# A 16-head, 64-dim cross-attention with query and key weights folded per head, and bias rows added by GpSimd

## The reference, cut to what matters

```
x = x + tanh(g_xattn[0]) * L0_xattn(layernorm(x), ctx)   # 16 heads of 8, biases
x = x + tanh(g_ffn[0])   * L0_ffn(layernorm(x))          # 8 experts, top 2
x = x + tanh(g_xattn[1]) * L1_xattn(layernorm(x), ctx)   # 16 heads of 64
x = x + tanh(g_ffn[1])   * L1_ffn(layernorm(x))          # 8 small experts, thresholded
x = x + tanh(g_xattn[2]) * L2_xattn(layernorm(x), ctx)   # one head of 128
x = x + tanh(g_ffn[2])   * L2_ffn(layernorm(x))          # 8 experts, top 1
x = x + tanh(g_xattn[3]) * L3_xattn(layernorm(x), ctx)   # 16 heads of 8, biases
x = x + tanh(g_ffn[3])   * L3_ffn(layernorm(x))          # ternary weights
```

```
def L1_xattn(x, context):            # HEADS = 16, DIM_HEAD = 64
    q, k, v = x @ Wq, context @ Wk, context @ Wv       # 128x1024, 96x1024, 96x1024
    sim = einsum('bhid,bhjd->bhij', heads(q), heads(k)) * 64 ** -0.5
    out = einsum('bhij,bhjd->bhid', softmax(sim), heads(v))
    return merged(out) @ Wo + bo
```

## Time and profile before

| what | value |
|---|---|
| median of 3 runs | 857.47 us (855.55 to 860.73) |
| the profiled execution, its own time | 856.33 us |
| its span, first to last instruction | 854.5 us |
| mean granted TensorE clock | 0.901 |
| PE, PEld busy | 712.4 us (83%), 599.3 us (70%) |
| DVE, ACT, POOL busy | 473.5 us (55%), 401.1 us (47%), 304.7 us (36%) |
| chain that ended last: PE, DVE, issue, DMA, ACT, POOL | 65%, 16%, 5%, 5%, 5%, 3% |
| `heads8(0)`, `experts(0)` on PE | from about 22 us, 140 to 263.7 us |
| `heads64` on PE | 263.7 to about 492 us |
| `heads8(1)` on PE | about 687 to 806 us |

### The profile page before, as it was taken

How to read it: one execution, slowest core, us unless ns; L and a number is a source line. 1 busy time by engine, 2 the same in 40 slices (tenths; PEclk the granted TensorE clock), 3 DMA queues, 4 the chain that set the end, 5 groups by cost and what they waited for, 6 DMA issues and landing times.

```text
span 854.5 us, 17772 instructions
## 1 busy us (share of the span) xinstructions
PE 712.4 (83%) x6653; PEld 599.3 (70%) x6653; DVE 473.5 (55%) x1439; ACT 401.1 (47%) x965; POOL 304.7 (36%) x256
## 2 busy tenths in 40 slices
PE   4698896499895898898999998885699749998873
PEld 3477783399895797796988843653699647787663
DVE  5365768432236767656656577446433425668662
ACT  4465440156562563554546565311346635555640
POOL 4443513556243371220312247203153354243121
PEclk9999996599997999999999999865699858999997
DMA  6442833756862010000000020004357444320000
GB/s 170 127 109 61 239 109 109 220 150 201 245 197 71 16 33 4 1 2 0 2 1 2 1 75 1 1 1 134 92 164 224 128 101 126 86 63 2 2 26 25
DMA packets 60544, 70.88 MB, mean 83 GB/s; under 512 B 7036, under 2 KB 40717, under 8 KB 60461
## 3 DMA queue, kind: packets, MB, share of 16 engines
q1 hardware_dynamic: 57389, 63.45, 26.2%
q0 software_dynamic: 3072, 6.30, 2.6%
HBM read 48.82 MB, written 20.91 MB: 82 GB/s over the span
## 4 chain that ended last, share of the span: by engine, by line
PE 65%; DVE 16%; issue 5%; DMA 5%; ACT 5%; POOL 3%; SPq 0%; POOLq 0%; DVEq 0%; ACTq 0%
PE banks L1375 7%; PE banks L1391 6%; PE banks L1460 4%; PE banks L1192 4%; PE banks L1469 3%; PE banks L1106 3%; PE banks L1215 3%; PE banks L1480 3%; PE banks L1064 3%; PE banks L1204 3%; PE banks L1170 3%; PE banks L1065 2%; PE banks L1066 2%; PE banks L1513 2%; DVE xn L1712 2%
## 5 line engine op out<-in xcount | busy, mean ns | idle before, releaser
L914 ACT ACTIVATE hT<-banks,wup 128x128 f32<-128x128 f32 x304 | 86.5, 368 | 75.8 <-PE banks L1375 74.9
L844 ACT ACTIVATE pT<-banks 77x512 f32<-77x512 f32 x128 | 69.0, 589 | 61.9 <-PE banks L1192 61.6
L582 POOL TENSOR_TENSOR kbd<-k,const 96x1248 fp32r<-96x1248 f32 x32 | 72.8, 2284 | 59.5 <-PE banks L1192 56.9
L620 POOL TENSOR_TENSOR sh<-sh,rd 128x616 f32<-128x616 f32 x32 | 38.9, 1216 | 134.1 <-DVE rd L1750 134.1
L1375 PE MATMUL banks<-xTs,wup 128*128 128x128 f32 x608 | 84.3, 285 | 2.0 <-ACT hT L914 1.2
L660 POOL DMA_INDIRECT xs<-xn,slot x48 | 47.3, 985 | 101.7 <-DVE slot L1996 48.4
L1391 PE MATMUL banks<-wd,hT 128*128 x608 | 80.8, 276 | 0.5 <-ACT hT L914 0.4
L1375 PEld LDWEIGHTS banks<-xTs,wup 128*128 128x128 f32 x608 | 77.7, 201 | 2.7 <-issue 2.5
L1391 PEld LDWEIGHTS banks<-wd,hT 128*128 128x128 f32 x608 | 74.0, 192 | 1.0 <-issue 0.9
L2103 DVE COPY ysb<-banks 128x128 f32<-128x128 f32 x76 | 22.1, 291 | 93.6 <-PE banks L1391 93.5
L562 POOL TENSOR_TENSOR rstd<-vv,const 128x4 f32<-128x4 f32 x24 | 24.4, 1016 | 128.6 <-DVE vv L1702 126.8
(11 more groups left out here) (318 smaller groups left out, 1643.0 us busy)
## 6 DMA issues: line engine op xcount, KB each, us to landing
wup<-in_up SPq DMA_DIRECT2D x76, 258.0 KB, 3.4
q<-queries SPq DMA_DIRECT2D x24, 256.0 KB, 4.6
queries<-qc SPq DMA_DIRECT2D x8, 512.0 KB, 2.6
wd<-in_down SPq DMA_DIRECT2D x8, 512.0 KB, 5.9
ys<-ysb SPq DMA_DIRECT2D x16, 256.0 KB
k<-keys SPq DMA_DIRECT2D x24, 156.0 KB, 3.5
...
```

Source lines behind the costliest of these rows:

```text
L582: pool.tensor_tensor(kbd[b % NB8][0:96, :, :, :].bitcast(F32R), kb, m, ALU.mult).then_inc(h8.kbd, 1)
L844: act.activation(pT[b % 2][0:SK, u, :], ps[0:SK, 2 + u % 2, :], ACT.Exp, scale=D8 ** -0.5)\
L914: ins = act.activation(hT[T % 3][:, c, :], ps[:, T % 2, c * P:c * P + P], func, bias=wup[T % NW][:, HID + c:HID + c + 1])
```

## The change

It has four parts.

1. **Folded weights.** Scores are x Wq_h (c Wk_h)^T = x (Wq_h Wk_h^T) c^T. In the second half of `experts(0)`, `folded_weights(j)` of PE, behind tiles 3 and 10, makes for each of the 16 heads the 96x128 product from transposed raw weights (64 deep, float32; even heads lie in partitions 0 to 63, odd ones in 64 to 127). ACT copies the high parts out behind tiles 5, 6, 12, 13, DVE the low parts behind 7, 8, 14, 15. POOL now splits only the value weights, at move 8.
2. **Folded keys.** `folded_keys(g, part)` makes for each head a 128x312 block from the folded weights and the context (three float32r matmuls), without x. Even heads are copied out by DVE, odd ones by ACT, into one of two buffers k1. Group 0's stand at the stage's start; group g+1's stand in step 0 of group g, behind each half of `own_values`. The scores of a unit are one float32 matmul of 128x312, with the plain transposed x as weights. q1, its matmuls and copies, xhi, xlo and `front_c` of this stage, and the memset of k1 go. k1 of the next group must be copied out before the scores of batch 1.
3. **Order of `heads64`.** The group's `front` runs one group ahead, behind the last `project`; nothing stands any more between the last `values` and `project`. On DVE `last_rows` (group 0) and `front_a` stand at step 4 ahead of `add`, `front_b` at step 5.
4. **Bias rows.** The ones-row matmul of `project` goes in both `heads8` runs (32 in all) and in `heads64` (16). POOL multiplies the bias row by tanh(g) once for each layer and adds it to a group's x (`bias_rows`, a 128x512 add, 12 in all) once that group's xn is written; DVE's first `add` of a group waits for it. The bias is loaded broadcast to all partitions.

```diff
-PLAIN = (*range(3 * NG, 5 * NG),)
+PLAIN = (*range(2 * NG, 5 * NG),)
...
-            for i, n in enumerate(("q", "k", "v")):
-                rows = P if i == 0 else DC
-                sp.dma_start(l1raw[0:rows, i, :], a["L1_xattn_W" + n]).then_inc(ld.l1raw, 16)
+            sp.dma_start(wqT[:, :, :], a["wqT"]).then_inc(ld.l1raw, 16)
+            sp.dma_start(wkT, a["wkT"]).then_inc(ld.l1raw, 16)
+            sp.dma_start(l1raw[0:DC, 2, :], a["L1_xattn_Wv"]).then_inc(ld.l1raw, 16)
...
+    def bias_rows(g, n, rows):
+        pool.wait_ge(fr.xn, upto(n))
+        xt = x[:, GB * g:GB * g + GB, :]
+        pool.tensor_tensor(xt, xt, rows.unsqueeze(1).to_broadcast([P, GB, D]), ALU.add).then_inc(h8.b, 1)
...
+            if b == 0:
+                if run == 0:
+                    pool.wait_ge(su.tanh, 1)
+                pool.tensor_scalar(rows, rows, tg[:, 0, 3 * run:3 * run + 1], None, ALU.mult).then_inc(su.zero, 1)
+                pool.wait_ge(su.zero, 4 + 2 * run)
+                bias_rows(0, NG * phase, rows)
+            if b % GB == 1 and b // GB < NG - 1:
+                bias_rows(b // GB + 1, NG * phase + b // GB + 1, rows)
...
-                if hh == 1 and m in (4, 8, 12):
-                    split_l1(m // 4 - 1)
+                if hh == 1 and m == 8:
+                    split_values()
...
-    pool.wait_ge(mo.tr, BASE[2])
-    pool.wait_ge(mo.scat, moves(2))
-    pool.memset(k1[:, :, :, :, :], 0.0).then_inc(su.scratch, 1)
+    rsqrt_front(2 * NG + 1)
     for g in range(NG):
-        rsqrt_front(g + 2 * NG + 1)
+        if g == 0:
+            pool.wait_ge(ld.l1raw, 96)
+            pool.tensor_scalar(bo[:, :], bo[:, :], tg[:, 0, 1:2], None, ALU.mult).then_inc(su.zero, 1)
+            pool.wait_ge(su.zero, 5)
+        bias_rows(g, 2 * NG + g, bo[:, :])
         for b in range(GB):
             for half in range(2):
                 if g == 0:
                     collect(1, 2 * b + half, 8)
                 normalise(h64, g, b, half)
-    rsqrt_front(3 * NG + 1)
+        rsqrt_front(g + 2 * NG + 2)
...
+        def folded_keys(g, part):
+            for h in range(8 * part + 1, 8 * part + 9, 2):
+                act.wait_ge(h64.kmm, H * g + h + 1)
+                copy(k1[g % 2][:, h, :, :].rearrange("p b t -> p (b t)"), ps[:, 2 + h % 4, 0:GB * SP]).then_inc(h64.q, 1)
...
-            pe.matmul(o_, oT8[:, :], a_raw[:, 3 * P:4 * P], start=True, stop=False)
-            pe.matmul(o_, const[0:1, C_ONE:C_ONE + P], a_raw[0:1, 4 * P:5 * P], start=False, stop=True)\
-                .then_inc(h8.y, 1)
+            pe.matmul(o_, oT8[:, :], a_raw[:, 3 * P:4 * P], start=True, stop=True).then_inc(h8.y, 1)
...
+    def folded_weights(j):
+        pe.wait_ge(ld.l1raw, 64)
+        if j == 0:
+            pe.wait_ge(mo.xb, 4)
+        else:
+            pe.wait_ge(su.lo, NG + 2)
+        for h in range(8 * j, 8 * j + 8):
+            rows = slice(64 * (h % 2), 64 * (h % 2) + 64)
+            at = h % 8 // 2 * P
+            ins = pe.matmul(ps[0:DC, 2 + h % 2, at:at + P], wkT[rows, h // 2, :], wqT[rows, h // 2, :],
+                            start=True, stop=True)
+        ins.then_inc(h64.qmm, 1)
     def heads64():
-        pe.wait_ge(wr.l1, 3)
-        def blocks(g, between):
-            pe.wait_ge(fr.lo, upto(g + 2 * NG))
+        pe.wait_ge(wr.l1, 1)
+        pe.wait_ge(su.lo, 2 * NG)
+        pe.wait_ge(mo.scat, moves(2))
...
+        def folded_keys(g, part):
             ct = tuple(c_[0:DC, GB * g:GB * g + GB, :].rearrange("p b t -> p (b t)") for c_ in (chi, clo))
-            for c in range(C1):
-                if c >= 4:
-                    pe.wait_ge(h64.q, 8 * g + c - 3)
-                split3(ps[:, c % 4, :], tuple(w_[:, 0, c * P:c * P + P] for w_ in l1w), xs).then_inc(h64.qmm, 1)
-                if c >= 2:
-                    pe.wait_ge(h64.k, 8 * g + c - 1)
-                split3(ps[:, 4 + c % 2, 0:GB * SP], tuple(w_[0:DC, 1, c * P:c * P + P] for w_ in l1w), ct)\
-                    .then_inc(h64.kmm, 1)
-            between()
+            for h in range(8 * part, 8 * part + 8):
+                if h % 8 >= 4:
+                    pe.wait_ge(h64.q if h % 2 else h64.k, 8 * g + h // 2 - 1)
+                elif g:
+                    pe.wait_ge(h64.v, 8 * g - 7 + 4 * part + h % 8)
+                elif part:
+                    pe.wait_ge(h64.q if h % 2 else h64.k, h // 2 - 1)
+                split3(ps[:, 2 + h % 4, 0:GB * SP],
+                       tuple(w_[0:DC, h // 8, (h % 8) * P:(h % 8) * P + P] for w_ in l1w), ct).then_inc(h64.kmm, 1)
         def own_values(g, part):
             for i in range(4 * part, 4 * part + 4):
-                if i >= 4:
+                if i >= 4 and g < NG - 1:
+                    pe.wait_ge(h64.q if i % 2 else h64.k, 8 * (g + 1) + i // 2 + 1)
+                elif i >= 4:
                     pe.wait_ge(h64.v, 8 * g + i - 3)
                 split3(ps[0:SK, 2 + i % 4, :], tuple(c_[0:DC, GB * g + i // 2, 0:SK] for c_ in (chi, clo)),
                        tuple(w_[0:DC, 2, 512 * (i % 2):512 * (i % 2) + 512] for w_ in l1w)).then_inc(h64.vmm, 1)
+            if g == 0 and part == 0:
+                front(2 * NG + 1)
+            if g < NG - 1:
+                folded_keys(g + 1, part)
         def scores(g, b, u):
             if b == 0 and u == 0:
                 pe.wait_ge(h64.k, 8 * g + 8)
                 pe.wait_ge(h64.q, 8 * g + 8)
-                pe.wait_ge(fr.lo, upto(g + 2 * NG + 1))
+                pe.wait_ge(fr.lo, upto(g + 2 * NG))
             if b == 1 and u == 0:
                 pe.wait_ge(h64.v, 8 * g + 8)
+                if g < NG - 1:
+                    pe.wait_ge(h64.k, 8 * g + 16)
+                    pe.wait_ge(h64.q, 8 * g + 16)
+                pe.wait_ge(fr.lo, upto(g + 2 * NG + 1))
                 if g == NG - 1:
                     pe.wait_ge(mx.d, 1)
-            for i in range(2):
-                ins = pe.matmul(ps[:, u % 2, 2 * i * SP:2 * (i + 1) * SP], q1[:, 2 * u + i, b * P:b * P + P],
-                                k1[:, 2 * u + i, b, :, :].rearrange("p h t -> p (h t)"), start=True, stop=True)
-            return ins
+            return pe.matmul(ps[:, u % 2, 0:4 * SP].rearrange("p (h t) -> p h t", h=4),
+                             xT[(g + 2 * NG) % 2][:, b * P:b * P + P], k1[g % 2][:, 4 * u:4 * u + 4, b, :],
+                             start=True, stop=True)
...
             pe.wait_ge(ld.l1raw, 96)
             pe.wait_ge(h64.oT, 2 * (4 * g + b) + 2)
             for c in range(C1):
-                pe.matmul(ps[:, 6, 0:P], oT[:, c, :], wo1[:, c, :], start=(c == 0), stop=False)
-            pe.matmul(ps[:, 6, 0:P], const[0:1, C_ONE:C_ONE + P], bo[:, :], start=False, stop=True)\
-                .then_inc(h64.y, 1)
-        blocks(0, lambda: None)
-        front(2 * NG + 1)
+                ins = pe.matmul(ps[:, 6, 0:P], oT[:, c, :], wo1[:, c, :], start=(c == 0), stop=(c == C1 - 1))
+            ins.then_inc(h64.y, 1)
+        folded_keys(0, 0)
+        folded_keys(0, 1)
+        front(2 * NG)
         for g in range(0, NG - 1):
-            attend(h64, g, scores, own_values, values, project, lambda between: blocks(g + 1, between))
+            attend(h64, g, scores, own_values, values, project)
...
-    def attend(hs, G, add, prepare=None, between=None):
+    def attend(hs, G, add, folded_keys, between, prepare=None):
-            if i == GB and between:
+            if i == GB:
                 between()
-                wait_done(dve, "ff", 1)
...
+                    if i == 0 and G < NG - 1:
+                        folded_keys(G + 1, pair)
...
-        def blocks(g, between):
-            n = g + 2 * NG + 1
-            gn = next_group(g)
-            front_a(gn, n)
-            for c in range(C1):
-                if c == 0:
-                    dve.wait_ge(su.scratch, 2)
-                dve.wait_ge(h64.kmm, 8 * g + c + 1)
-                for par in range(2):
-                    rows = slice(64 * par, 64 * par + 64)
-                    ins = dve.tensor_copy(k1[rows, c, :, par, :],
-                                          ps[rows, 4 + c % 2, 0:GB * SP].rearrange("p (b t) -> p b t", b=GB))
-                ins.then_inc(h64.k, 1)
-                if c == 1:
-                    front_b(gn, n)
-            between()
+        def folded_keys(g, part):
+            if g == 1 and part == 0:
+                dve.wait_ge(mo.ys, 16 * stores(2))
+            for h in range(8 * part, 8 * part + 8, 2):
+                dve.wait_ge(h64.kmm, H * g + h + 1)
+                dve.tensor_copy(k1[g % 2][:, h, :, :].rearrange("p b t -> p (b t)"), ps[:, 2 + h % 4, 0:GB * SP])\
+                   .then_inc(h64.k, 1)
         def add(g, b):
             dve.wait_ge(h64.y, 4 * g + b + 1)
+            if b == 0:
+                dve.wait_ge(h8.b, NG + g + 1)
             add_to_x(g * GB + b, 1, ps[:, 6, 0:P], tg[:, 0, 1:2], h64.x)
-        blocks(0, lambda: None)
-        front_c(2 * NG + 1)
+        def stats(g):
```

(14 more changed lines are left out.)

85 lines of the change are left out of this document (54 added, 31 removed).

## The result

The changed kernel takes 819.61 us (median of 4 runs, 817.99 to 821.95) against 857.53 for the kernel before (4 runs): ratio 0.956, 95% interval 0.951 to 0.960. The forecast was 821.4. The profiled execution took 817.99 us, 38.3 less than the profiled one of before (856.33).

A forecast was written before the change was run, and what follows sets the result against it. PE was taken as the bound, busy 83% of the span. Terms -9.8 - 33.0 + 20.4 + 0.5 - 5.3 + 1.4 - 11.0 + 1.9 sum to -34.9 from the profiled 856.33 us, giving 821.4 us, range 809 to 838.

The forecast's parts named there:

- start of `heads64`: Experts' end to first scores: folded keys start without x, xn takes 1.1 us; -9.8 us, bounds -7.5 and -12.
- three passages: Between a group's last `values` and the next scores: only oT copy wait, `project` and transposes stay; -33.0 us.
- three first batches (with the moved transposes): Groups 0 to 2, step 0: 48 key matmuls each, +20.4 us; group 1's transposes moved into group 0, +0.5 us.
- other batches: bias matmul, statistics ahead of `add`: `heads64`: 13 bias matmuls of 0.41 us gone, -5.3 us; longer wait for `add` in group 0's step 4, +1.4 us.
- bias matmul, `heads8`: Both `heads8` runs: 32 matmuls of 0.42 us gone, 25 counting fully; -11 us, bounds -5 and -15.
- experts: folding, earlier row moves: Experts' stage: 16 folding matmuls cost +3.8 us, the wait for rows nearly goes, -1.9 us; together +1.9 us.
- The rival of the copies: First batches: DVE and ACT bring keys late, PE stands some 4 us more in each of three; 833 us, chance 0.13.
- The rival that this matmul was hidden: `heads8`: ACT and DVE chains do not pass through the ones-row matmul, so -11 becomes 0; 832 us, chance 0.08.
- the bound of 1.9: Experts' stage: folding matmuls in different row groups run at the same time, costing 1.9 us instead of 3.8.
- GpSimd's adds: Bias adds and row scalings on GpSimd hold up VectorE's xn; at most 15.2 us, 837 us, chance 0.09.
- The rivals of the low clock (slower than before): `heads64`: added idle pieces keep PE's clock low; half the stage low would give 911 us; chance 0.02.
- a change that does less: Whole kernel: less gain than said, or an unseen wait takes most back; within 0.5% of before, chance 0.02.

The follow-up runs named there:

- run 5: Changed kernel with GpSimd's 4.25 us memset put back later in the 64-dim stage, behind a wait for the 16th folded key; ratio to the kernel before 0.961.
- run 4: Changed kernel with GpSimd's 4.25 us memset back at its old place in GpSimd's order, over the second key buffer; ratio to the kernel before 0.959.
- Run 6: Changed kernel with the next group's folded keys made between last `values` and last `project` instead of in the first batch; ratio to the kernel before 0.955.
- Run 3: Kernel before with only the bias part: GpSimd adds the bias rows, the 48 1-deep matmuls gone; 833.75 us, ratio to the kernel before 0.978.
- Runs 1 and 2: Changed kernel with a zero-adding matmul in each of 48 projections, 1-deep in the first, 128-deep in the second; ratios to the kernel before 0.991 and 0.965.
- run 7: Changed kernel with all 16 folding matmuls reading partitions 0 to 63, leaving the odd heads' weights out; ratio to the kernel before 0.956.

## Why the prediction was right

Term by term, profiled execution against profiled execution:

| term | predicted | measured |
|---|---|---|
| start of `heads64` | -9.8 | -10.5 |
| three passages | -33.0 | -30.1 |
| three first batches (with the moved transposes) | +20.9 | +18.9 |
| other batches: bias matmul, statistics ahead of `add` | -3.9 | -4.4 |
| bias matmul, `heads8` | -11.0 | -16.2 |
| experts: folding, earlier row moves | +1.9 | +2.9 |
| stages not touched | 0 | +1.2 |
| sum | -34.9 | -38.3 |

The time is near the forecast (819.6 against 821.4) partly by luck: four terms gave 8.4 us more than they were put down for and three gave 5.1 less, and much of that cancels.

**Start.** Right in mechanism and near in size. DVE's first copy of a key was ready 5.3 us behind the experts' end, 5.4 by the prediction. Keys did not begin at once, though: PE waited 1.42 us for the last `ysb`, and so the wait for the copy was 1.89 us, not 3.7; together it is 3.3 us of idle time, with some 3.3 us at the low clock behind it. That xn takes 1.1 us since the memset is gone fits run 5, where a memset over xn makes it 4.51; run 4 does not speak against it, since its memset began when xn was over. How much of the 10.5 us is due to the faster xn and how much to keys that no longer wait for x was not run.

**Passages.** The second and third came as said (3.1 and 4.9 against 3.1 and 4.7). The first was 5.8: the term took 1.9 us for `project` and left out what the stop ahead of `values` does to the clock. The kernel before had this too: behind its stop of 2.09 us the first queries' matmuls stand 0.43 us apart for some 3 us, and 0.23 later.

**First batches.** "Copies keep up but for the last": 0.72 us for it, with 0.6 predicted. Run 6 takes the keys out again and finds 6.8 us of matmuls each. The rival of the copies falls. The term is 2 us too large mainly for the third of them, which gave +5.0 us: before it took 10.6 us instead of 9.0, part of it at the low clock, and the changed kernel's has no such stretch.

**Other batches.** In group 0, where DVE's statistics stand ahead of `add`, the wait grew from 2.09 to 3.42 us (+1.33; +1.4 was predicted). Each `project` there gave 0.59 us, not 0.41. Unforeseen: the last `values` of group 3 wait 1.42 us for an `add`, 0.85 before.

**`heads8`** is the term that was mis-sized, and its bound of -15 was missed in this trace too. The matmul was priced from its own start to that of the next instruction, 0.42 us, and in 25 of 32 places; that leaves out what it does to the instruction ahead of it. PE's timeline of one batch of `heads8`, before and then after:

```profile
63.35 0.49 PE L1223 MATMUL banks<-a_raw,oT 128*128 128x128 f32 x2
63.77 0.48 PE L1224 MATMUL banks<-a_raw,const 1*128 1x128 f32 x2
64.19 0.55 PE L1170 MATMUL banks<-kbd,q 96*128 96x312 f32 x2
```

```profile
61.44 0.49 PE L1252 MATMUL banks<-a_raw,oT 128*128 128x128 f32 x2
61.69 0.53 PE L1199 MATMUL banks<-kbd,q 96*128 96x312 f32 x2
```

From `project` to the next scores 0.84 us became 0.25. So some 0.5 us went in every batch, not 0.42 in three of four: 16.2 us over 32. Run 3, with the same edits in `heads8`, gives 14.7, just inside the bound; its first `heads8` takes 100.98 us where the changed kernel's takes 99.19, so 1.8 us of this term are the spread between executions. Both are above the 11 us of the forecast. Runs 1 and 2 show why the matmul's own 0.42 us misleads. The rival that this matmul was hidden falls with the same numbers.

**Experts.** Folding is 2 x 1.0 us, not 3.8: the bound of 1.9 was right, and with it what the Trainium skill says of row groups (TensorE: Matmul & The Clock Gate, Part 3; run 7). The other half of the term failed: of the 2.27 us for the slots' rows only 0.25 went. PE's timeline:

```profile
206.32 0.33 PE L1392 MATMUL banks<-const,xsb 128*128 128x128 f32 x1 [0.99 <-DMA xsb<-xs]
215.42 0.33 PE L1392 MATMUL banks<-const,xsb 128*128 128x128 f32 x1 [1.03 <-DMA xsb<-xs]
```

GpSimd's last move is earlier by 9.55 us, 8.7 of them from `heads8`, so in the stage by 0.8 only; the rest of the rows now ends a wait of its own. Folding and these waits make +1.75; of the other 1.1 us, 0.55 is a wait of PE at 191.93 with no releaser shown, and the rest was not found.

**GpSimd's adds.** Timeline of GpSimd and VectorE at the first passage:

```profile
317.73 1.27 POOL L602 TENSOR_TENSOR x<-x,bo 128x512 f32<-128x512 f32 x1
...
317.78 2.08 DVE L1766 TENSOR_SCALAR xn<-x,mv,rstd 128x128 f32<-128x128 f32 x4 [0.90 <-POOL rstd L566]
```

The collision is there: xn takes 2.08 instead of 1.11, and PE's transposes come 3.9 us after its end. It is so in all three passages (2.06 in the other two, with 2.9 us to spare), and the other nine adds meet no xn. The rival had the mechanism and no price.

The rivals of the low clock (slower than before) and of a change that does less are out by the result.

**Stages not touched** cost 1.2 us, which is what the other terms leave of the sum; by the traces 4.2 us were lost between `heads64` and the second `heads8` and 3.2 won at the end of the kernel. The lost part lies in the one-head layer and the routing behind it, with the same waits and a granted clock of 0.72 and 0.50 instead of 0.75 and 0.55. Why, in either place, was not tried.
